# Weights of three feed-forward layers turned and split beside the first two attention halves instead of in the set-up program

## The reference, cut to what matters

```python
x = x + tanh(g_xattn[0]) * _L0_xattn_ref(_layernorm(x), ctx, ctx, ...)
x = x + tanh(g_ffn[0])   * _L0_ffn_ref(_layernorm(x), ...)
x = x + tanh(g_xattn[1]) * _L1_xattn_ref(...)
x = x + tanh(g_ffn[1])   * _L1_ffn_ref(...)   # 4 experts: silu(x @ w1[e]) * (x @ w3[e]) @ w2[e], w1 and w3 [4, 128, 512]
x = x + tanh(g_xattn[2]) * _L2_xattn_ref(...)
x = x + tanh(g_ffn[2])   * _L2_ffn_ref(...)   # 8 experts: W1 and W2 [8, 352, 128], W3 [8, 128, 352]
x = x + tanh(g_xattn[3]) * _L3_xattn_ref(...)
x = x + tanh(g_ffn[3])   * _L3_ffn_ref(...)   # 8 experts: W_experts [8, 128, 128]
```

## Time and profile before

| what | value |
|---|---|
| time before, median of 3 runs (lowest to highest) | 1064.07 us (1063.49 to 1065.72) |
| the profiled execution's own time | 1065.34 us |
| its span, first to last instruction | 1063.6 us |
| PE, PEld, DVE, ACT, POOL busy in the span | 85%, 57%, 67%, 43%, 10% |
| mean granted TensorE clock | 0.951 of full |

### The profile page before, as it was taken

One profiled execution on the slowest core, in us unless ns is written; L12 is line 12 of the kernel. 1 busy time (PEld: TensorE's weight loads), 2 busy tenths in 40 slices (PEclk: granted clock), 3 DMA queues, 4 the chain that ended last, 5 costly groups with the idle time before them and its releaser, 6 DMA issues.

```text
span 1063.6 us, 14472 instructions
## 1 busy us (share of the span) xinstructions
PE 905.5 (85%) x4795; PEld 608.3 (57%) x4795; DVE 709.5 (67%) x2190; ACT 457.7 (43%) x1101; POOL 104.8 (10%) x175
## 2 busy tenths in 40 slices
PE   2459899997877878978999999999999888889967
PEld 2434544543343555665667677677667666667744
DVE  0962652639295695895848858658856787877845
ACT  0514455567767656566354263253153222212200
POOL 3100000004031130130000101000100200000000
PEclk9669999998898999999999999999999999999987
DMA  9400000000000000000000000000000000000000
GB/s 260 144 2 1 1 1 1 1 1 1 0 1 1 1 1 1 1 2 1 1 1 2 1 1 1 1 1 1 1 1 1 1 1 11 1 11 1 1 11 10
DMA packets 12066, 12.72 MB, mean 12 GB/s; under 512 B 3759, under 2 KB 7897, under 8 KB 11993
## 3 DMA queue, kind: packets, MB, share of 16 engines
q10 hardware_dynamic: 5536, 8.04, 2.5%
q1 hardware_dynamic: 6072, 3.24, 1.1%
q0 software_dynamic: 384, 0.53, 0.3%
HBM read 10.75 MB, written 1.05 MB: 11 GB/s over the span
## 4 chain that ended last, share of the span: by engine, by line
PE 57%; DVE 23%; ACT 6%; issue 5%; POOL 2%; POOLq 0%; ACTq 0%; DVEq 0%
PE bank L1608 10%; PE bank L1596 6%; PE bank L1518 5%; PE bank L1598 5%; PE bank L1597 5%; PE bank L1533 4%; PE bank L1403 4%; DVE x L1313 3%; DVE nm L1153 3%; DVE hb L1297 3%; DVE hb L1288 2%; ACT PTs L957 2%; PE bank L1573 2%; DVE x L1277 2%; PE bank L1356 2%
## 5 line engine op out<-in xcount | busy, mean ns | idle before, releaser
L994 ACT ACTIVATE hb<-bank 96x512 f32<-96x512 f32 (+1 forms) x160 | 95.0, 594 | 244.8 <-PE bank L1598 244.1
L1608 PEld LDWEIGHTS bank<-m_w,hb 128*128 128x128 f32 (+1 forms) x1280 | 165.9, 194 | 22.5 <-issue 4.9
L1596 PE MATMUL bank<-parts,m_w_lo 128*96 128x512 f32 (+1 forms) x320 | 151.9, 475 | 29.9 <-DVE hb L1288 20.5
L1608 PE MATMUL bank<-m_w,hb 128*128 128x128 f32 (+1 forms) x1280 | 175.4, 281 | 2.2 <-DVE hb L1288 2.0
L1297 DVE SCALAR_TENSOR_TENSOR hb<-hb,bank 96x512 f32<-96x512 f32 (+1 forms) x160 | 109.0, 682 | 93.8 <-ACT hb L994 93.0
L1598 PE MATMUL bank<-parts,m_w_hi 128*96 128x512 f32 (+1 forms) x320 | 127.2, 398 | 0.0
L1597 PE MATMUL bank<-parts,m_w_hi 128*96 128x512 f32 (+1 forms) x320 | 127.0, 397 | 0.0
L1288 DVE TENSOR_TENSOR hb<-hb,bank 96x512 f32<-96x512 f32 (+1 forms) x160 | 109.7, 686 | 8.6 <-PE bank L1598 3.0
L1533 PE MATMUL bank<-Qs,KT 112*77 112x512 f32 x192 | 94.5, 517 | 10.9 <-ACT PTs L957 8.8
L1596 PEld LDWEIGHTS bank<-parts,m_w_lo 128*96 128x96 f32 (+1 forms) x320 | 59.0, 184 | 78.1 <-DVE hb L1288 32.6
L1029 DVE RECIPROCAL rden<-bank 128x16 f32<-128x16 f32 x48 | 12.2, 255 | 122.3 <-PE bank L1356 122.3
(11 more groups left out here) (271 smaller groups left out, 1525.9 us busy)
## 6 DMA issues: line engine op xcount, KB each, us to landing
m_w<-in_L_ffn_w_dram ACTq DMA_DIRECT2D x2, 1024.0 KB, 11.5
nat_m<-in_L_ffn_W_dram ACTq DMA_DIRECT2D x1, 1408.0 KB, 16.8
x<-in_x_dram SPq DMA_DIRECT2D x4, 256.0 KB, 8.4
out_dram<-x SPq DMA_DIRECT2D x4, 256.0 KB, 2.0
f_out<-in_L_ffn_Wout_dram POOLq DMA_DIRECT2D x8, 64.0 KB, 7.7
m_w<-in_L_ffn_W_experts_dram ACTq DMA_DIRECT2D x1, 512.0 KB, 17.2
ctxn<-in_ctx_dram SPq DMA_DIRECT2D x4, 38.5 KB
Wq<-in_L_xattn_Wq_dram SPq DMA_DIRECT2D x2, 64.0 KB
```

Source lines behind the costliest of these rows:

```text
L994: act.activation(hb[n % 3][0:m, :], bank[UP[u, n]][0:m, :], ACT.Tanh, scale=0.5).then_inc(*chunk_act.up(u, n))
L1596: pe.matmul(dst, w_lo, x_hi, start=True, stop=False)
L1608: op = pe.matmul(bank[7][:, t * P:(t + 1) * P], hb[n % 3][0:m, t * P:(t + 1) * P], wd, start=i == 0 and t == 0, stop=ends_expert(k, n) and ...
```

## The change

The large weights of layers 1 to 3 are loaded into the memory of their own low part (`parts()` lays the raw tile and the low part at one address), and the first program no longer touches them. The second program has new steps `prepare()` at the head of the feed-forward track: 30 pieces of work (`WORK`) and two empty steps. The first 18 steps are merged with A0, the other 14 and the five of F0's preparation with A1. A piece "raw" (8 of them, layer 1) is one ACT rounding and one DVE subtraction of 512 columns; a piece "split" (14, layers 2 and 3) is up to four transposes on PE into bank 4, 5 or 6, one ACT rounding and one DVE subtraction of up to 512 columns; a piece "turn" (8, W3 of layer 2, transposed from and back to the same tile) is three transposes and two ACT copies. ACT's part stands one step behind PE's, DVE's two steps.

In the first program the transfers are dealt out anew: SP starts 26 small ones and then four large ones; ACT starts 42 small ones (among them `x`, `ctxn` and the masks, which were on SP) and then the three large ones of layers 2 and 3. POOL's subtraction is gone, and the key masks of all streams are made in one pass.

```diff
+        def parts(name, shape):
+            with nc.sbuf_tensor(name + "_raw", shape, F32) as raw:
+                pass
+            low = sb(name + "_lo", shape, F32R)
+            return [sb(name + "_hi", shape, F32R), low], raw[:]
...
             def _(sp):
...
+                for raw, n in zip(raw_m1, ("w1", "w3")):
+                    sp.dma_start(raw, a[f"L1_ffn_{n}"].rearrange("e d f -> d e f")).then_inc(*landed["m1_" + n].up("all", by=16))
+                sp.dma_start(raw_w3, a["L2_ffn_W3"].rearrange("e m n -> m e n")).then_inc(*landed["m2_w3"].up("all", by=16))
+                sp.dma_start(m1_w2[:], a["L1_ffn_w2"].rearrange("e (c p) d -> p e c d", p=P)) \
+                    .then_inc(*landed["rest"].up("all", by=16))
-                for name in ("small", "rest", "gates"):
+                for name in ("small", "side", "gates"):
                     sp.wait_ge(*landed[name].at("all"))
...
             def _(act):
...
                 for i, (_, row) in enumerate(groups):
-                    if i == first_turn:
-                        act.wait_ge(*landed["m1"].at("all"))
-                        for raw, w in ((raw_w1, m1_w1), (raw_w3, m1_w3)):
-                            act.activation(w[0][:], raw, ACT.Copy).then_inc(*keptA.up("m1", w[0].name))
...
-                    if i in split:
-                        act.wait_ge(*turned.at(i))
-                        for src, dst, at in row:
-                            op = act.activation(dst[0], bank[i % 8][:, at:at + P], ACT.Copy)
-                        op.then_inc(*keptA.up(i))
-                    elif i % 2:
+                    if i % 2:
                         act.wait_ge(*turned.at(i))
...
-                pool.tensor_tensor(m1_w3[1][:], raw_w3, m1_w3[0][:].bitcast(F32), ALU.subtract) \
-                    .then_inc(*m1_low.up("m1_w3"))
...
+                for i in range(len(groups)):
+                    dve.wait_ge(*kept(i))
+                dve.wait_ge(*landed["small"].at("all"))
...
-                for b in range(STREAMS):
-                    if b:
-                        dve.wait_ge(*masks_ready.at("all", b - 1))
-                    dve.tensor_copy(mk[b][:, 0:1], mk_i[b][:, 0:1])
...
+                dve.tensor_copy(mks[:, :, 0], mk_i[:, 0, :])
...
+    PREP_BANK = (4, 5, 6)
+    WIDE = 4
+    WORK = [("raw", w, raw, n, e) for w, raw, n in ((m1_w1, raw_m1[0], "w1"), (m1_w3, raw_m1[1], "w3")) for e in range(MOE1)]
+    WORK += [("split", w, raw, n, c, min(WIDE, raw.shape[1] // P - c))
+             for w, raw, n in ((m2_w1, raw_m2[0], "m2_w1"), (m2_w2, raw_m2[1], "m2_w2"), (m3_w, raw_m3, "m3"))
+             for c in range(0, raw.shape[1] // P, WIDE)]
+    WORK += [("turn", e) for e in reversed(range(MOE2))]
+    PREPS = len(WORK) + 2
+    PREPS_A = 18
...
-        yield from "A" * len(weights_a(("A", 0)))
-        yield from merged(weights_a(("A", 1)), [1.0] * steps_pre("F0"))
+        yield from merged(weights_a(("A", 0)), [1.0] * PREPS_A)
+        yield from merged(weights_a(("A", 1)), [1.0] * (PREPS - PREPS_A + steps_pre("F0")))
...
         @block.scalar
         def _(act):
+            def prepare():
+                yield
+                for n, (what, *of) in enumerate(WORK):
...
+                        act.wait_ge(*weight_turned.at(n))
+                        act.activation(w[0][:, c * P:(c + many) * P], bank[PREP_BANK[n % 3]][:, 0:many * P], ACT.Copy) \
+                            .then_inc(*weight_high.up(n))
...
         @block.vector
         def _(dve):
+            def prepare():
+                yield
+                yield
+                for n, (what, *of) in enumerate(WORK):
...
+                        dve.wait_ge(*weight_high.at(n))
+                        dve.tensor_tensor(w[1][:, part], bank[PREP_BANK[n % 3]][:, 0:many * P], w[0][:, part].bitcast(F32), ALU.subtract) \
+                            .then_inc(*weight_low.up(n))
...
+            def prepare():
+                for n, (what, *of) in enumerate(WORK):
+                    if what != "raw":
+                        b = PREP_BANK[n % 3]
+                        free(b)
+                        if what == "split":
+                            w, raw, load, c, many = of
+                            pe.wait_ge(*landed[load].at("all"))
+                            for i in range(many):
+                                op = pe.transpose(bank[b][:, i * P:(i + 1) * P], raw[:, (c + i) * P:(c + i + 1) * P], ident[:])
+                            reader[b] = (weight_low, n)
...
+                if u[1] == STREAMS and half == "F":
+                    pe.wait_ge(*weight_high.at(len(WORK) - 1))
```

More of the change, by code:

```diff
@@ L192, in build @@
         m3_rb = sb("m3_rb", [1, MOE3])
-        m3_w = [sb(f"m3_w_{part}", [P, MOE3 * P], F32R) for part in ("hi", "lo")]
+        m3_w, raw_m3 = parts("m3_w", [P, MOE3 * P])
         m3_b = sb("m3_b", [MOE3, P])
@@ L253, in build @@
             quad_b = tmp("quad_b", [P, 4, J])
-            landed = {n: sig("landed_" + n) for n in ("small", "gates", "turn", "m2_w1", "m2_w2", "m2_w3", "m3", "m1", "rest", "mask", "f0", "rows")}
+            landed = {n: sig("landed_" + n) for n in ("small", "side", "gates", "turn", "late_turn", "m2_w1", "m2_w2", "m2_w3", "m3", "m1_w1", "m1_w3",
+                                                      "rest", "mask", "f0", "rows")}
             zeroed = sig("zeroed")
@@ L276, in grouped @@
                 groups.append((load, row))
-            def split_parts(load, nat, w, count=NCH):
-                grouped(load, [(nat[:, c, :], [part[:, c * P:(c + 1) * P] for part in w]) for c in range(count)])
-                return list(range(len(groups) - -(-count // 4), len(groups)))
-            split = split_parts("m2_w1", nat_m1, m2_w1)
-            split += split_parts("m2_w2", nat_m2, m2_w2)
-            split += split_parts("m3", nat_e, m3_w, MOE3)
-            first_turn = len(groups)
             grouped("turn", [(nat1[0][:], Wq[1][:]), (nat1[1][:], Wk[1][:]), (nat1[2][:], Wv[1][:]), (nat3x[:], W3x[:])])
@@ L288, in build @@
                              (natwo[:], Wo[1][:])])
-            grouped("turn", [(nat_t1[:], t_w1T[:]), (nat_t2[:], t_w2T[:]), (nat_r[:, 0, :], m2_router[:]),
+            grouped("late_turn", [(nat_t1[:], t_w1T[:]), (nat_t2[:], t_w2T[:]), (nat_r[:, 0, :], m2_router[:]),
                              (nat_r[:, 1, :], m3_router[:]), (nat_f0[:, 0, :], f0_cols[:, 0, :]),
                              (nat_f0[:, 3, :], f0_cols[:, 1, :]), (nat_f0[:, 2, :], f0_cols[:, 2, :])])
-            last_turn = len(groups) - 1
             grouped("mask", [(mf[:, t, :], mask_k[:, t * P:(t + 1) * P]) for t in range(T)])
-            m2_last = len(groups)
-            grouped("m2_w3", [(nat_m3[:, e, o:o + w], m2_w3[0:w, e, i, :]) for e in range(MOE2)
-                              for i, (o, w) in enumerate(pieces(F2))])
             def kept(i):
-                return (keptA if i % 2 and i not in split else keptD).at(i)
+                return (keptA if i % 2 else keptD).at(i)
             block = pro.enter_context(nc.Block())
@@ L390, in _ @@
                         op.then_inc(*keptA.up(i))
+                act.wait_ge(*landed["gates"].at("all"))
+                act.activation(gates_col[:], graw[:], ACT.Tanh)
             @block.gpsimd
@@ L536, in _ @@
                     op.then_inc(*turned.up(i))
-                last = len(groups) - 1
-                for i in range(max(0, last - 7), last + 1):
+                for i in range(len(groups)):
                     pe.wait_ge(*kept(i))
-                pe.wait_ge(*landed["small"].at("all"))
+                for name in ("small", "side"):
+                    pe.wait_ge(*landed[name].at("all"))
                 pe.matmul(bank[0][:, 0:1], f0_wout[:], f0_b2[:], start=True, stop=True)
@@ L658, in main @@
         "gates_ready").split())
+    weight_turned, weight_high, weight_low = (sig(n) for n in "weight_turned weight_high weight_low".split())
     (chunk_psum, chunk_act, chunk_silu, chunk_ready, ffn_psum,
@@ L810, in _ @@
         def _(pool):
+            def prepare():
+                for _ in range(PREPS):
+                    yield
             def pre(u):
@@ L1567, in body @@
                 xf = xff[s]
+                if u[1] == STREAMS and half == "F":
+                    pe.wait_ge(*weight_high.at(len(WORK) - 1))
+                    pe.wait_ge(*weight_low.at(max(n for n, (what, *_) in enumerate(WORK) if what != "turn")))
+                    pe.wait_ge(*landed["rest"].at("all"))
                 if k == "F0":
```

251 lines of the change are left out of this document (128 added, 123 removed).

## The result

The changed kernel takes 1055.02 us (median of 6 runs, 1051.96 to 1057.18), the kernel before 1063.78 beside it (6 runs, 1060.64 to 1065.84). The ratio is 0.9915, 95% interval 0.989 to 0.9939: faster by 0.85%. The forecast was 1055 and faster.

The account below looks back on a forecast made before the run. It took a chain on ACT and DVE, with ACT's start behind its large transfers, to bound the first program's end. Starting A0 22.3 us earlier, less 12.8 us for pieces, gave -9.5 us: 1055 us, range 1049 to 1062.

Parts of the forecast that it names:

- Step 1: First program: ACT starts 42 small transfers at 0.43 us each, 17.9 us, so its large ones start at about 18.7.
- Step 2: First program: ACT's queue is held 13.0 us by its three large loads (bounds 10.9 to 18.5), free at 31.7.
- Steps 3 to 5: First program's tail: ACT's table load and groups until 34.1, DVE's widening and scaling until 38.0, biases and masks until 42.9.
- A0 until the end of its blocks: Eight layer-1 pieces add 2.8 us: four DVE subtractions of 0.62 between reductions, and about 0.3 before the last `Qs`.
- A0's heads: Six "split" pieces add 4.5 us: 2.7 from PE's transposes, the rest from six ACT stops of 0.3.
- Between the halves and A1's blocks: From A0's heads to the end of A1's blocks: PE turns and DVE subtractions, less 1.15 for moved statistics, add 3.3 us.
- A1's heads: Five "turn" pieces add 2.2 us: PE 1.3, ACT's stops 1.5, less 0.59 as `xnf`'s transposes leave.
- the likeliest case: A0 starts between 40 and 47 and 9 to 17 us are added; 1050 to 1060 us, chance 0.70.
- late release: Rival, first program: ACT is released late, second program starts at 48.4, gain only 4.0 us, 1060; chance 0.10.
- Lockstep: Rival: turned pieces pay PE, ACT and DVE parts one after another, 1.83 us each; slower, 1084 or 1078; chance 0.06.
- the clock: Rival: idler PE in A0 or A1 lowers its clock, at most 3.3 us each half; gain 2.9, 1061; chance 0.07.

Follow-up runs that it names:

- e12: Changed kernel with DVE making all small copies, bias inputs loaded first under their own semaphore, and all large loads moved behind the barrier; 1037.68 us, one run.
- e1: Changed kernel, but DVE copies all four small groups of the first program out of the banks and ACT none; 1046.26 us, ratio 0.9828 to before.
- e2: Changed kernel, but ACT's three large loads are started by SP as the first thing of the second program; 1042.65 us, ratio 0.9796 to before.
- e11: The changed kernel itself, unaltered, measured again beside later runs; 1053.62 us, ratio 0.9907 to before.
- e6: Changed kernel with ACT's copies of the 22 turned pieces done twice, first into a tile not yet in use; 1055.76 us, one run.
- e8: Kernel before, with only F0's preparation moved behind 14 empty steps, where the change puts it; 1061.45 us, one run.
- e5: Changed kernel with every PE transpose of the 22 turned pieces issued twice; 1062.83 us, one run.
- e7: Changed kernel with DVE's subtraction done twice in all 22 pieces that have one; 1067.36 us, one run.
- e4: Changed kernel with layer 2's W1 and W2 pieces first and layer 1's eight pieces behind them, in A0's heads; 1051.49 us, ratio 0.988 to before.

## Why the prediction was right, and where its numbers were not

That the time came out within 0.1 us is luck: the gain forecast for the first program was 4.7 us too large, the cost forecast for the pieces 5.0 too large, and the two cancelled; the six runs alone spread over 5 us. The mechanism on both sides is the one forecast. Step by step:

- **Step 1, ACT's 42 small issues, large ones from 18.7 on:** mis-sized. They took 21.1 us for 17.9, and the large ones began at 22.23. The count was right, the price was an average over other transfers (e12).
- **Step 2, 13.0 us held by the large ones:** 14.0 (22.23 to 36.26), within the bounds 10.9 to 18.5. All queues together moved 358 GB/s from 20 to 30 us, with SP's loads among them. The rule of the Trainium skill that the prediction weighed here ("DMA: Bandwidth & Descriptors", section "Issuing engines are not separate DMA queues"), that a second engine's transfers share the same DMA engines, agrees with that: 358 GB/s at most, against 348 in the earlier trace rows. That step 2 would by this rule come out near its upper ends did not happen; 14.0 is nearer to the lower one.
- **Steps 3 to 5, 11.2 us from ACT's release to A0:** 36.26 to 47.61, 11.35. Right; the chain was the same as before, as read.
- The gain was thus 17.6 instead of 22.3: 3.5 of the difference in step 1, 1.0 in step 2, 0.2 in the tail. The mechanism (ACT's queue as the gate) is shown by e1 and e2, which take it away in two ways and gain 9 and 12 us against after.
- **A0 until the end of its blocks, 2.8:** 2.2 (2.53 in the blocks, -0.33 ahead of them, where the clock's rise differs from run to run; in e11 S to T0 is 0.9 longer, so 2.2 to 3.1). From one reduction row to the next a subtraction took 0.61 (61.50 to 62.11) for the 0.62 forecast.
- **A0's heads, 4.5:** 1.7. Both parts were too dear. A row of four transposes lasts 0.60 us, but the next instruction of PE starts 0.44 after the row's start (75.12 and 75.56): the rows overlap. Four pieces and a half are 2.0 us at that price, not 2.7. And six stops of 0.3 by ACT have no room: PE was idle 0.54 us in the whole stage, less than the 0.99 of before, and its wait of 0.60 for `PTs` became 0.18. A doubled copy (e6) does cost 1.4 there.
- **Between the halves and A1's blocks, 3.3:** 3.4, and right part by part. The six subtractions cost 3.70 for 3.5, the statistics that left the chain gave 1.18 for 1.15, and ahead of `x` 0.8 were added for 0.9. e8 adds that the 1.15 are worth something only because pieces fill the room.
- **A1's heads, 2.2:** 0.5. The same two prices were too dear as in A0's; what each of them made here was not measured apart.

Of the signs named in advance, these came: the statistics at 47.61 (41 to 48), the reductions with four subtractions in 8.79 us (60.22 to 69.01; 8.8), everything behind A2 earlier by 9.8 (9 or 10). A0's heads grew by 1.7 and not by 3 to 6. And one sign of being wrong came too: ACT's issue of the large loads ended at 36.26, "much after 32".

The rivals: the start of the second program at 47.61 lies between the likeliest case (40 to 47) and late release (48.4), so ACT was in fact released nearly as late as that rival said, though mostly through its small issues and not through shared bandwidth; with 12.8 us added this start would have given about 1059. Lockstep is refuted by the 7.8 us and by e5. Behind its first rise the clock did not fall in A0 and A1 of after, but does with 2.4 us more in the blocks (e7), and did once in e4.

The gain grew from 9.8 us at A2 to 12.8 over the two profiled spans. From A2's first query product on the kernels run the same instructions, and the rest of the span is 914.9 in before, 911.5 in e8, which is before again, 911.9 in after and 913.9 in e11, which is after again; in e5 and e7, whose edits end before it, it is even 918.4. So 3 us there are scatter and not a third effect. The mean clock of the whole span does not explain it: e8 has 0.948, before 0.951. The medians differ by 8.8.

## What to carry to other kernels

Engines that compute should not start large transfers ahead of small work that others wait for; here 14 us of issuing held three engines, and taking it away gained 12 us, where the change itself gained 9. When a wait is removed, look at once for the one under it: shared semaphores ("all small ones landed") hid a second wait of 13 us that cost nothing until the first was gone. Price an inserted instruction by the distance to the next one's start and not by the row's length, and price it at the place where it goes, in a gap or on the chain.
